# Two-layer cross-attention kernel: project only the first four batches ahead of the first attention, and the other twelve inside it

## The chip, the cores and the metric

One Trainium2 chip, one core. The metric is the device time of one execution of the whole program, in microseconds, lower is better. The engines are TensorE (PE), VectorE (DVE), ScalarE (ACT), GpSimd (POOL) and SyncE (SP); SP computes nothing here and issues most DMAs. A `q` behind a name (SPq, ACTq) means that the engine's queue issues something, a DMA above all.

## The reference

Sixteen batches of 128 tokens with 128 features go through cross-attention with biases (layer 0, 16 heads of 8), a mixture of eight experts, a masked causal cross-attention (layer 1), and a ternary feed-forward part. Only the first layer's attention and what stands ahead of it are touched:

```python
xn = (x - mean) / sqrt(var + eps)          # over the 128 features
q = split_heads(xn @ Wq.T + bq)
k = split_heads(ctx @ Wk.T + bk)
v = split_heads(ctx @ Wv.T + bv)
scores = einsum('bhqd,bhkd->bhqk', q, k) / sqrt(8)
probs = softmax(scores)
x = x + merge_heads(einsum('bhqk,bhkd->bhqd', probs, v)) @ Wo.T + bo
```

The products q·k are wanted in float32 accuracy while TensorE runs bf16. So every projection is split into three bf16 parts: the first is its rounding, the second the rounding of what is left (`rest`), the third what is left then.

## The kernel before

The program is five blocks one after the other, each with a program of its own for each engine; an engine enters a block only when all have left the one before: `context` (line 443), `attention` for layer 0 (line 709), `experts`, `attention` for layer 1, `ternary_ffn`. The order of the work in each is written out by hand.

**`context`** works by groups g of four batches (512 tokens). UNITS lists eight units: the keys and the queries of each group. TensorE projects keys (L655) from the transposed context `ctx_t`, turns the normalised tokens (L636), projects values (L643) and queries (L667). ScalarE copies a turned tile (L684), writes the first part of a unit (L696) and the second part (L689). VectorE measures the tokens (L578), normalises them (L594), forms `rest` (L601), adds the values' bias (L587); for the first queries it also makes parts two and three (L611, L613). GpSimd takes the root (L553) and makes the third part (L558). SyncE stores the parts into `k_dram` (five copies of 128 KB for a unit of keys, since parts one and two are stored twice) and `q_dram` (three), and loads the rows of batches 0 and 1 back (`load_half`, L110 and L113). Three units are stored in this block, the other five at places inside the attention (`LATE`). All weights, those of layer 1 too, are loaded at its start.

**`attention`** runs in steps b from -2 to 17, in the same order on each engine; four slots of `k_rows` and `q_rows` hold the rows of four batches. A step has four quarters q of four heads. In step b TensorE makes, by quarters, the scores of batch b+2 (L868), of which VectorE takes maxima (L958, and a split of them into bf16 parts, L965 to L971), and the shifted scores of batch b (L885), which ScalarE exponentiates (L1040). Behind quarter 0 stand the products with the values of batch b-1 (L899) and the turning of the maxima of batch b+1 (L906). ScalarE copies these (L1052) and SyncE lays them into three rows of `q_rows` by a DMA (`lay_maxima`, L795); the shifted scores of that batch wait for it. The output of batch b-2 is turned, projected (L921, L925) and added to x (L984). Rows of batch b+4 are loaded once the shifted scores of batch b have freed the slot:

```python
def load(b, r):
    for half in range(2):
        sp.wait_ge(shifted, (b - SLOTS) * NQ + (half + 1) * NQ // 2)
        load_half(sp, c, b, r, half)
    lay_maxima(b - 2, (r - 2) % SLOTS)
```

GpSimd puts the values of batch b into `v_aug` (`fill`, L1093), ahead of L899 of that batch. Behind its step 1 it adds the output's bias to all of x (L1115), and VectorE waits for that (`bias_added`) before its step 2.

**Semaphores around the change.** `stored` (here `first_stored`, `parts_stored`, `late_stored`, `last_stored`) stands at 16 per DMA landed; SyncE waits for it before it loads rows of that group. `third_ready` counts third parts, `copied` first parts, `rest_ready` what is left, `second_ready` second parts.

## Time and profile before

| | us |
|---|---|
| time, median of 3 runs | 433.83 (432.37 to 436.69) |
| time of the profiled execution | 434.39 |
| its span, from the first instruction to the last | 432.7 |
| outside the span | 1.69 |

Times of single instructions below are microseconds from the start of the span. The mean granted clock of TensorE over the span is 0.924 of full speed (2.4 GHz); the lower of its two levels is 1.2 GHz. Of the span about 38 us are the context phase and some 96 us the first attention.

### The profile page before, as it was taken

How to read it: one execution, taken by the hardware profiler on the slowest of the kernel's cores; microseconds unless marked ns; L12 is line 12 of the kernel's file. 1: busy time of each engine (PE TensorE's matmuls, PEld its weight loads, DVE VectorE, ACT ScalarE, POOL GpSimd, SP SyncE). 2: the span in 40 equal slices, each digit the busy share in tenths (PEclk: the TensorE clock that was granted, in tenths of full speed). 3: DMA queues.
4: the chain of work that ended last, by engine and by line, in shares of the span. 5: the costliest groups of instructions: out<-in, count | busy, mean ns of one | idle time of the engine just before them, and what ended most of it. 6: DMA issues, size and time to landing. Idle time of an engine off the chain costs nothing. (4 is left out here: it accounts for less than half of the span.)

```text
span 432.7 us, 10420 instructions
## 1 busy us (share of the span) xinstructions
PE 359.2 (83%) x3434; PEld 258.3 (60%) x3434; DVE 288.3 (67%) x905; ACT 224.6 (52%) x420; POOL 90.2 (21%) x163
## 2 busy tenths in 40 slices
PE   2684779887877999999999999799899999756654
PEld 0452667776753677677767777566677676534433
DVE  6765768998946553663442443687789799367993
ACT  2152436665654745434343344055556656648993
POOL 7335131020211102101001001133333343310000
PEclk9886769999996999999999999889999999857996
DMA  7664954433144001630170100113443331000111
GB/s 215 138 157 111 226 165 129 130 117 111 55 124 148 2 2 40 126 80 2 36 208 12 36 0 0 37 31 104 122 127 113 101 100 28 3 1 1 32 30 37
DMA packets 54100, 34.98 MB, mean 81 GB/s; under 512 B 38744, under 2 KB 46256, under 8 KB 54064
## 3 DMA queue, kind: packets, MB, share of 16 engines
q1 hardware_dynamic: 44032, 31.43, 26.8%
q10 hardware_dynamic: 10032, 3.08, 3.0%
q8 instruction: 20, 0.33, 0.3%
q14 instruction: 16, 0.13, 0.1%
HBM read 24.60 MB, written 9.44 MB: 79 GB/s over the span
## 5 line engine op out<-in xcount | busy, mean ns | idle before, releaser
L1040 ACT ACTIVATE probs<-ps_e 128x512 f32<-128x512 f32 x128 | 74.6, 594 | 54.2 <-PE ps_e L885 49.7
L958 DVE TENSOR_REDUCE neg<-ps_s 128x4 f32<-128x512 f32 x128 | 85.1, 684 | 21.6 <-PE ps_s L868 20.1
L1286 DVE SCALAR_TENSOR_TENSOR x_all<-ps_ym,c_g,x_all 128x128 f32 (+1 forms) x128 | 36.0, 344 | 63.2 <-PE ps_ym L1381 63.0
L1381 PEld LDWEIGHTS ps_ym<-w,hid 128*128 128x128 f32 x512 | 60.8, 192 | 9.2 <-issue 6.7
L868 PE MATMUL ps_s<-k_rows,q_rows 96*128 96x128 bf16 x512 | 54.2, 234 | 10.6 <-DVE neg L958 4.9
L1381 PE MATMUL ps_ym<-w,hid 128*128 128x128 f32 x512 | 62.2, 276 | 0.0
L1371 PE MATMUL ps_h<-tok_t,w 128*128 (+1 forms) x128 | 62.1, 608 | 0.0
L1488 ACT ACTIVATE hid<-ps_h,b 128x512 f32<-128x512 f32 x64 | 43.1, 684 | 35.4 <-PE ps_h L1371 34.0
L868 PEld LDWEIGHTS ps_s<-k_rows,q_rows 96*128 96x128 bf16 x512 | 40.1, 104 | 24.1 <-issue 10.0
L885 PE MATMUL ps_e<-q_rows,k_rows 128*128 128x128 bf16 x512 | 51.2, 226 | 3.8 <-DMA q_rows<-neg_t 3.3
L885 PEld LDWEIGHTS ps_e<-q_rows,k_rows 128*128 128x128 bf16 x512 | 37.0, 101 | 9.1 <-DMA q_rows<-neg_t 3.9
L899 PE MATMUL ps_pv<-probs,v_aug 128*32 128x128 f32 x1024 | 36.5, 285 | 0.0
L1371 PEld LDWEIGHTS ps_h<-tok_t,w 128*128 128x128 f32 x128 | 22.6, 195 | 20.1 <-issue 14.9
L1093 POOL TENSOR_TENSOR v_aug<-v_all,zero 128x128 f32<-128x128 f32 x32 | 14.8, 463 | 88.4 <-PE ps_pv L899 87.2
L864 PE MATMUL ps_s<-upper,identb 128*128 128x512 bf16 x64 | 25.8, 403 | 4.6 <-PEq L1138 2.0
L899 PEld LDWEIGHTS ps_pv<-probs,v_aug 128*32 128x32 f32 x1024 | 27.0, 113 | 4.1 <-issue 0.4
L1052 ACT ACTIVATE neg_t<-ps_n 48x128 bf16<-48x128 bf16 x32 | 8.6, 269 | 35.3 <-PE ps_n L906 35.3
L1718 PE MATMUL ps_tf<-ident,gr 128*128 128x128 f32 x64 | 11.3, 303 | 14.2 <-ACT gr L1672 14.2
L925 PE MATMUL ps_y<-attn_w,oo_t 128*128 128x128 f32 x64 | 16.2, 336 | 7.5 <-ACT oo_t L1057 6.8
L984 DVE TENSOR_TENSOR x_all<-ps_y,x_all 128x128 f32<-128x128 f32 (+1 forms) x32 | 9.2, 287 | 16.7 <-PE ps_y L925 16.4
L1102 POOL TENSOR_SCALAR_AFFINE_SELECT probs<-probs 128x512 f32<-128x512 f32 x32 | 20.0, 625 | 0.0
L1045 ACT ACTIVATE o_t<-ps_pv 128x512 f32<-128x512 f32 x32 | 18.6, 580 | 2.1 <-PE ps_pv L899 2.0
(200 smaller groups left out, 555.7 us busy)
## 6 DMA issues: line engine op xcount, KB each, us to landing
k_rows<-k_dram SPq DMA_DIRECT2D x32, 144.0 KB
q_rows<-q_dram SPq DMA_DIRECT2D x32, 144.0 KB
k_rows<-k_dram SPq DMA_DIRECT2D x16, 288.0 KB
q_rows<-q_dram SPq DMA_DIRECT2D x16, 288.0 KB
k_dram<-parts SPq DMA_DIRECT2D x35, 128.0 KB, 2.5
w<-in_w SPq DMA_DIRECT2D x16, 128.0 KB, 2.7
q_dram<-parts SPq DMA_DIRECT2D x15, 128.0 KB, 2.2
q_dram<-parts ACTq DMA_DIRECT2D x9, 128.0 KB, 3.2
```

Source lines behind the costliest of these rows:

```text
L864: pe.matmul(ps_s[:, q % 2, :], identb[:], c["upper"][:].unsqueeze(1).to_broadcast([P, HQ, P]), start=True, stop=False, skip_group_check=True)
L868: last = pe.matmul(ps_s[:, q % 2, j * P:(j + 1) * P], q_rows[0:ROW_MAX, r, h, :], k_rows[0:ROW_MAX, r, h, :], start=(layer == 0), stop=Tru ...
L885: last = pe.matmul(ps_e[:, q % 2, j * P:(j + 1) * P], k_rows[:, r, h, :], q_rows[:, r, h, :], start=not masked, stop=True, skip_group_chec ...
L899: last = pe.matmul(ps_v[VW * j:VW * (j + 1), q * P:(q + 1) * P], v_aug[:, s, q * HQ + j, :], probs[:, s, q, j * P:(j + 1) * P], start=True ...
L958: dve.tensor_reduce(neg[:, s, q * HQ:(q + 1) * HQ], ps_s[:, q % 2, :].rearrange("p (h k) -> p h k", h=HQ), AX_X, ALU.max, negate=True).the ...
L1040: act.activation(probs[:, s, q, :], ps_e[:, q % 2, :], ACT.Exp, scale=SCALE).then_inc(exp_done, 1)
L1045: act.activation(o_t[:, s, :], ps_v[:], ACT.Copy).then_inc(ot_ready, 1)
L1102: pool.affine_select(out=probs[:, s, q, :], in_=probs[:, s, q, :], compare_op=ALU.is_ge, fill=0.0, base=0, pattern=[[0, HQ], [1, P]], chan ...
L1286: dve.scalar_tensor_tensor(out=batch_of(x_all, g * G + j), in0=ps_y[:, e % 2, j * D:(j + 1) * D], scalar=c_g[:, j, e:e + 1], in1=batch_of( ...
L1371: pe.matmul(ps_h[:, m, :], w1[:, e, m * P:(m + 1) * P], tok_t[:, bass.ds(g * GT, GT)], start=True, stop=True).then_inc(h_done, 1)
L1381: last = pe.matmul(ps_y[:, e % 2, j * D:(j + 1) * D], hid[:, (e % 2) * M + m, j * P:(j + 1) * P], w2[:, e, m, :], start=(m == 0), stop=(m ...
L1488: act.activation(hid[:, (e % 2) * M + m, :], ps_h[:, m, :], ACT.Gelu, bias=b1[:, e * M + m:e * M + m + 1]).then_inc(h_ready, 1)
```

## The change

A class `Projections` (`pr`) holds the tensors, semaphores and steps of the projection, so that they live through `context` and the first `attention`. `context` now does the keys and queries of group 0, the values of groups 0 and 1, and the projection of the keys of group 1. The rest is spread over the attention: TensorE does four products ahead of step -2 into banks that the attention doesn't use yet (`ps_e`, `ps_pv`, `ps_y`, `ps_o`), and turns or projections of queries between quarters; ScalarE copies each late unit out of its bank twice (its first part, and in float32 into `rest`), GpSimd subtracts (`leave`) and makes the third part, ScalarE the second. The late units are numbered m = 0 to 5: keys of groups 1, 2, 3, queries of groups 1, 2, 3.

The queries of a group are stored by one DMA of 384 KB in place of three of 128 KB. The rows of batches 1 to 7 are loaded whole, by two DMAs in place of four. The values' bias is added in `fill` and no longer by VectorE. Layer 1's attention weights and the mask go from the start of `context` to the end of SyncE's attention program.

```diff
+LATE_UNITS = (("k", 1), ("k", 2), ("k", 3), ("q", 1), ("q", 2), ("q", 3))
+WHOLE = 2 * SLOTS
...
+    def copy_full(self, act, m, bank):
+        kind, g = LATE_UNITS[m]
+        self.copy_first(act, kind, g, m + 3, bank)
+        wait(act, self.third_ready, m - 3)
+        act.activation(self.rest[:, (m + 2) % 4, :], bank, ACT.Identity, bias=self.bias(kind)).then_inc(self.copied, 1)
...
+    def leave(self, pool, m):
+        kind, g = LATE_UNITS[m]
+        pool.wait_ge(self.copied, 2 + 2 * (m + 1))
+        pool.tensor_tensor(self.remainder(m + 2), self.remainder(m + 2), self.part(kind, g, 0), ALU.subtract)\
+            .then_inc(self.rest_ready, 1)
+    def second(self, act, m):
+        act.wait_ge(self.rest_ready, m + 1)
+        act.activation(self.part(kind, g, 1), self.remainder(m + 2), ACT.Copy).then_inc(self.second_ready, 1)
+    def third(self, pool, m):
+        pool.wait_ge(self.second_ready, m + 1)
+        pool.tensor_tensor(self.part(kind, g, 2), self.remainder(m + 2), self.part(kind, g, 1), ALU.subtract)\
+            .then_inc(self.third_ready, 1)
...
 # context, TensorE
+            pe.matmul(ps_p[:, 0, :], attn_w[:, 0, 1, :], ctx_t[:, 0:GT], start=True, stop=True).then_inc(pr.p_done, 1)
+            pr.turn(pe, 0, ps_x)
+            pr.queries(pe, 0, ps_p[:, 1, :])
+            pr.values(pe, 0, ps_v[:, 0])
+            pr.keys(pe, 1, ps_p[:, 2, :])
+            pr.values(pe, 1, ps_v[:, 1])
 # context, ScalarE
+            pr.copy_first(act, "k", 0, 1, ps_p[:, 0, :])
+            pr.copy_turned(act, 0, ps_x[:])
+            pr.copy_first(act, "q", 0, 2, ps_p[:, 1, :])
+            pr.copy_full(act, 0, ps_p[:, 2, :])
+            pr.copy_values(act, 0, ps_v[:, 0, :])
+            pr.copy_values(act, 1, ps_v[:, 1, :])
 # context, VectorE
+            pr.normalise(dve, 0, STAT_STEPS + 1)
+            pr.leave_first(dve, "k", 0, ps_p[:, 0, :])
+            dve.wait_ge(pr.x_in[1], 16)
+            dve.wait_ge(pr.x_in[2], 16)
+            pr.stats(dve, range(G, B))
+            pr.leave_first(dve, "q", 1, ps_p[:, 1, :])
 # attention, SyncE
+                pr.store_queries(sp, 0)
+                sp.wait_ge(pr.stored[0], 16 * (K_PARTS + 1))
+                for half in range(2):
+                    load_half(sp, c, 0, 0, half)
+                load_whole(sp, c, 1, 1)
+                load_whole(sp, c, 2, 2)
+                lay_maxima(0, 0)
+                load_whole(sp, c, 3, 3)
+                sp.wait_ge(pr.third_ready, 1)
+                pr.store_keys(sp, 1, (0, 3))
+                lay_maxima(1, 1)
+                pr.store_keys(sp, 1, (1, 4, 2))
+                sp.wait_ge(pr.third_ready, 4)
+                pr.store_queries(sp, 1)
+                sp.wait_ge(pr.stored[1], 16 * (K_PARTS + 1))
+                load(4, 0)
+                load(5, 1)
+                pr.store_keys(sp, 2, (0, 3))
+                load(6, 2)
+                pr.store_keys(sp, 2, (1, 4))
+                load(7, 3)
+                pr.store_keys(sp, 2, (2,))
+                sp.wait_ge(pr.third_ready, 5)
+                pr.store_queries(sp, 2)
+                sp.wait_ge(pr.stored[2], 16 * (K_PARTS + 1))
                 for b in range(2 * SLOTS, B):
+                    if b == last * G:
+                        sp.wait_ge(pr.stored[3], 16 * (K_PARTS + 1))
                     load(b, b % SLOTS)
...
+                for m, name in enumerate(("Wq", "Wk", "Wv", "Wo")):
+                    sp.dma_start(attn_w[:, 1, m, :], t["L1_" + name]).then_inc(gate_in, 16)
+                sp.dma_start(c["mask_dram"], c["mask_b"][:]).then_inc(gate_in, 16)
 # attention, TensorE: beside a quarter (step, quarter)
+                (-2, 1): lambda: pr.turn(pe, 2, bank_t),
+                (-1, 1): lambda: (pe.wait_ge(pr.copied, 2 + 2 * 3), pr.queries(pe, 2, bank_q[1])),
+                (-1, 3): lambda: pr.turn(pe, 3, bank_t),
+                (0, 1): lambda: (pe.wait_ge(pr.v_ready, NG), pr.queries(pe, 3, bank_q[2])),
 # attention, VectorE, ahead of its steps
+                pr.variance(dve, G, B, STAT_STEPS + 1)
+                for g in range(1, NG):
+                    pr.normalise(dve, g, 2 * (STAT_STEPS + 1) + (g > 1))
 # attention, ScalarE: behind steps -3, -2, -1 and 0
+            def first_copies():
+                pr.copy_full(act, 1, bank_k[0])
+                pr.copy_values(act, 2, bank_v[0])
+                pr.copy_turned(act, 1, bank_t[:])
+                pr.copy_full(act, 2, bank_k[1])
+                pr.copy_values(act, 3, bank_v[1])
+                pr.copy_full(act, 3, bank_q[0])
+                pr.second(act, 0)
+            def second_copies():
+                pr.copy_turned(act, 2, bank_t[:])
+                pr.second(act, 1)
+                pr.second(act, 2)
+            def third_copies():
+                pr.copy_full(act, 4, bank_q[1])
+                pr.copy_turned(act, 3, bank_t[:])
+            def fourth_copies():
+                pr.second(act, 3)
+                pr.copy_full(act, 5, bank_q[2])
+                pr.second(act, 4)
...
+                if also else {-3: first_copies, -2: second_copies, -1: third_copies, 0: fourth_copies,
+                              1: lambda: pr.second(act, 5), 2: lambda: store_last((0, 3)), 3: lambda: store_last((1, 4)),
+                              4: lambda: (store_last((2,)), pr.store_queries(act, 3))},
 # attention, GpSimd: ahead of its steps, then behind steps -2, 0 and 1
+                for m, later in ((0, 0), (1, 0), (0, 1), (2, 0), (1, 1), (2, 1)):
+                    if later:
+                        pr.third(pool, m)
+                    else:
+                        pr.leave(pool, m)
...
             def add_bias():
+                split_late(5)
+                pool.wait_ge(pr.xn_ready, B)
                 pool.tensor_tensor(x_all[:], x_all[:], c["row_bias"][:, 1, :].unsqueeze(1).to_broadcast([P, B, D]),
                                    ALU.add).then_inc(bias_added, 1)
...
+                else {-2: lambda: split_late(3), 0: lambda: split_late(4), 1: add_bias}, beside)
```

`split_late(m)` is `leave(m)` and then `third(m)`.

ScalarE, from the copy of batch 0's maxima to batch 1's second exponential (`probs0` is written by the exponentials, `neg_t0` by the copy of the maxima, `o_t0` by the copy of the sums). Before:

```order
L1052 ACTIVATE neg_t0<-ps_n0 48x128
L143 DMA k_dram<-parts 128x4x128 x5
L1040 ACTIVATE probs0<-ps_e0 128x512
L1052 ACTIVATE neg_t0<-ps_n0 48x128
L1040 ACTIVATE probs0<-ps_e0 128x512 x4
L1052 ACTIVATE neg_t0<-ps_n0 48x128
L1045 ACTIVATE o_t0<-ps_pv0 128x512
L1040 ACTIVATE probs0<-ps_e0 128x512 x3
```

And now:

```order
L1126 ACTIVATE neg_t0<-ps_n0 48x128
L263 ACTIVATE parts<-ps_e0,attn_bias 128x4x128
L272 ACTIVATE pr_rest<-ps_e0,attn_bias 128x512
L282 ACTIVATE pr_xn_t<-ps_o0 128x512
L1114 ACTIVATE probs0<-ps_e0 128x512
L1126 ACTIVATE neg_t0<-ps_n0 48x128
L1114 ACTIVATE probs0<-ps_e0 128x512 x3
L295 ACTIVATE parts<-pr_rest 128x4x128
L263 ACTIVATE parts<-ps_y0,attn_bias 128x4x128
L272 ACTIVATE pr_rest<-ps_y0,attn_bias 128x512
L295 ACTIVATE parts<-pr_rest 128x4x128
L1114 ACTIVATE probs0<-ps_e0 128x512
```

Four copies now stand between batch 0's last exponential and batch 1's first, and three ahead of batch 0's first.

GpSimd, from the clearing of `v_aug0` to the addition of the bias to x. Before:

```order
L1085 MEMSET v_aug0 128x1024
L1087 MEMSET v_aug0 128x32
L1093 TENSOR_TENSOR v_aug0<-v_all,zero 128x16x8 x3
L1115 TENSOR_TENSOR x_all<-x_all,row_bias 128x2048
L1093 TENSOR_TENSOR v_aug0<-v_all,zero 128x16x8 x4
```

And now:

```order
L1196 MEMSET v_aug0 128x1024
L1198 MEMSET v_aug0 128x32
L288 TENSOR_TENSOR pr_rest<-pr_rest,parts 128x512
L301 TENSOR_TENSOR parts<-pr_rest,parts 128x4x128
L1207 TENSOR_TENSOR v_aug0<-v_all,row_bias 128x16x8 x2
L288 TENSOR_TENSOR pr_rest<-pr_rest,parts 128x512
L301 TENSOR_TENSOR parts<-pr_rest,parts 128x4x128
L1207 TENSOR_TENSOR v_aug0<-v_all,row_bias 128x16x8
L288 TENSOR_TENSOR pr_rest<-pr_rest,parts 128x512
L301 TENSOR_TENSOR parts<-pr_rest,parts 128x4x128
L1236 TENSOR_TENSOR x_all<-x_all,row_bias 128x2048
L1207 TENSOR_TENSOR v_aug0<-v_all,row_bias 128x16x8 x4
```

The splits of the queries of groups 1, 2 and 3 (L288 and L301, m = 3, 4, 5) now stand ahead of the first `fill`, ahead of the third, and ahead of the addition to x.

SyncE's queue, in the changed kernel, from the rows of batch 7 to the maxima of batch 6 (`q_rows<-neg_t0` lays maxima). The whole rows of batch 7 are the first two rows, the halves of batch 8 stand behind the stores:

```order
L155 DMA k_rows<-k_dram 72x1x2048
L158 DMA q_rows<-q_dram 72x1x2048
L816 DMA q_rows<-neg_t0 3x16x128
L210 DMA k_dram<-parts 128x4x128
L214 DMA q_dram<-parts 128x12x128
L110 DMA k_rows<-k_dram 72x1x1024
L113 DMA q_rows<-q_dram 72x1x1024
L110 DMA k_rows<-k_dram 72x1x1024
L113 DMA q_rows<-q_dram 72x1x1024
L816 DMA q_rows<-neg_t0 3x16x128
```

Before, nothing stands between the maxima of batch 5 and the rows of batch 8. The two stores of group 2, and SyncE's wait for them, now stand there.

## Rows read from the trace of the kernel before

**Rows 1.** Windows of context and attention: length, busy us of five engines, clock, DMA, GB/s.
```profile
0.00:38.00 38.00, 19.40 (x66) 11.61 (x67) 23.78 (x62) 13.21 (x21) 18.22 (x31) 0.88 0.59 151
38.00:134.00 96.00, 76.16 (x1155) 61.76 (x1156) 75.51 (x236) 49.73 (x112) 18.20 (x25) 0.89 0.49 138
```

**Rows 2.** Timeline of the context phase: start, length, engine, line, what, count, idle before.
```profile
13.17 1.91 PE L667 MATMUL ps_p<-xn_t,attn_w 128*128 128x512 f32 x2
13.32 2.42 DVE L578 BATCH_NORM_STATS2 st_all<-x_all 128x6 f32<-128x128 f32 x12 [2.88 <-DMA x_all<-in_x]
...
19.18 1.49 SPq L143 DMA_DIRECT2D q_dram<-parts  x3
...
20.88 1.09 DVE L594 TENSOR_SCALAR xn<-x_all,mean,rstd 128x128 f32<-128x128 f32 x4
...
22.37 0.96 SPq L110 DMA_DIRECT2D k_rows<-k_dram  x1
...
26.31 2.88 DVE L594 TENSOR_SCALAR xn<-x_all,mean,rstd 128x128 f32<-128x128 f32 x4
...
27.91 1.12 PE L667 MATMUL ps_p<-xn_t,attn_w 128*128 128x512 f32 x2 [0.46 <-ACT xn_t L684]
...
35.32 2.26 POOL L558 TENSOR_TENSOR parts<-rest,parts 128x512 bf16<-128x512 f32 x2 [1.75 <-ACT parts L689]
...
37.93 1.01 PE L868 MATMUL ps_s<-k_rows,q_rows 96*128 96x128 bf16 x8 [3.93 <-PEq L448]
```

**Rows 3.** Groups on ScalarE, 0 to 80 us: a second part; count, busy us, mean ns.
```profile
L689 ACT ACTIVATE parts<-rest 128x512 bf16<-128x512 f32 x7 | 4.4, 625 | 1.2 <-DVE rest L601 1.1
```

**Rows 4.** Timeline of the first attention, from the first exponential to step 2.
```profile
46.84 0.60 ACT L1040 ACTIVATE probs<-ps_e 128x512 f32<-128x512 f32 x1 [3.98 <-PE ps_e L885]
...
49.51 0.60 ACT L1040 ACTIVATE probs<-ps_e 128x512 f32<-128x512 f32 x1 [0.26 <-PE ps_e L885]
...
51.76 0.80 SPq L110 DMA_DIRECT2D k_rows<-k_dram  x1
...
52.00 0.45 POOL L1093 TENSOR_TENSOR v_aug<-v_all,zero 128x128 f32<-128x128 f32 x1 [11.76 <-PE ps_pv L899]
...
52.41 4.51 POOL L1115 TENSOR_TENSOR x_all<-x_all,row_bias 128x2048 f32<-128x2048 f32 x1
...
54.53 2.42 DVE L965 CAST neg_parts<-neg 128x16 bf16<-128x16 f32 x1
...
55.67 0.40 PE L868 MATMUL ps_s<-k_rows,q_rows 96*128 96x128 bf16 x4 [1.68 <-DMA q_rows<-q_dram]
...
57.46 0.61 PE L885 MATMUL ps_e<-q_rows,k_rows 128*128 128x128 bf16 x4 [1.40 <-DMA q_rows<-neg_t]
...
57.99 0.68 DVE L958 TENSOR_REDUCE neg<-ps_s 128x4 f32<-128x512 f32 x1
...
61.01 0.63 PE L868 MATMUL ps_s<-k_rows,q_rows 96*128 96x128 bf16 x4
```

**Rows 5.** Windows, 58 to 63 us: length, busy us of five engines, clock, DMA, GB/s.
```profile
58.00:63.00 5.00, 5.00 (x56) 4.41 (x56) 2.34 (x5) 2.71 (x6) 0.46 (x1) 0.50 0.56 153
```

**Rows 6.** Timeline, steps 4 to 6: first shifted scores of steps 4 and 6; maxima laid.
```profile
68.48 0.39 PE L885 MATMUL ps_e<-q_rows,k_rows 128*128 128x128 bf16 x4
...
70.59 0.76 SPq L795 DMA_DIRECT2D q_rows<-neg_t  x1
...
75.07 0.76 SPq L795 DMA_DIRECT2D q_rows<-neg_t  x1
...
77.72 0.39 PE L885 MATMUL ps_e<-q_rows,k_rows 128*128 128x128 bf16 x4
```

**Rows 7.** The page, part 6: a store's DMA, its size, us from issue to landing.
```profile
q_dram<-parts SPq DMA_DIRECT2D x15, 128.0 KB, 2.2
```

**Rows 8.** Timeline, end of the attention: SyncE's last DMA, TensorE's first of the experts.
```profile
130.62 0.43 SPq L137 DMA_DIRECT2D w<-in_w  x1
...
133.54 1.08 PE L1348 MATMUL ps_q<-ident,tok_tk 128*128 128x128 f32 x4 [1.24 <-PEq L716]
```

431 lines of the change are left out of this document (212 added, 219 removed).

## The prediction

> **What bounds the kernel now.** I read the windows by stage first, then the timeline of the first 80 us engine by engine, then groups for durations, and the waits where the timeline showed gaps. The windows say how much the change can touch: 38 us of context and 96 us of attention [rows 1]. In the context no engine is full: VectorE, the busiest, works 23.8 of 38 us, TensorE 19.4. It is a chain. VectorE waits for the twelve later batches of x and measures them (13.32, 2.42 us) before it splits the first queries, stored from 19.18; the first rows are fetched from 22.37; GpSimd's last third parts end at 37.58, and only then can the attention begin, at 37.93 [rows 2]. Rows of batches 0 and 1 had long been fetched by then. The first exponential starts at 46.84. Steps 1 to 3 have waits of their own: TensorE waits for rows of batch 4 until 55.67, for batch 2's maxima until 57.46, VectorE for x until 57.99 [rows 4]. TensorE comes back at the low clock: 58 to 63 us shows a granted clock of 0.50 with TensorE busy for all 5 us [rows 5]. From 68.48 the attention has its pace: two steps take 77.72 - 68.48 = 9.24 us [rows 6], or 4.62 each, in which VectorE and TensorE are both nearly full. Time saved at the start counts only if it is still there at 68.48, and time lost after that is lost.
>
> **The change, step by step.** I carry five marks through it.
>
> 1. *Attention begins.* The first queries no longer wait behind the values, and VectorE's splitting ends near 17. Last to leave the context is now ScalarE, which copies group 1's keys twice and two banks of values. TensorE's products (two of 512 columns are 1.91 us at the low clock, 1.12 at the high one [rows 2]) give 19.8, between 18.5 and 20.5, against 37.9. But the first queries' store moves behind this point.
>
> 2. *First exponential.* Before, three query stores from 19.18 had landed when the rows were fetched at 22.37, 3.2 us [rows 2]. One DMA of the same 384 KB: 3.2 to 4, I take 3.6, so fetching starts at 23.4. A half fetched from 51.76 was there at 55.67, 3.9 us [rows 4]: scores at 27.3. TensorE's four products, a turn and a projection ahead of them end between 27 and 29.2, by the clock. Before, scores to exponential took 46.84 - 37.93 = 8.9 us [rows 2, 4]. It gets 0.8 longer: group 2's turning stands between quarters, and ScalarE reaches the copy of the maxima behind `second(2)`, which waits for GpSimd's three subtractions. 27.3 + 8.9 + 0.8 = 37.0 (36.2 to 39), 9.8 ahead of before.
>
> 3. *VectorE goes on into step 2.* Here the 9.8 us go. Before, the exponential at 46.84 was followed by VectorE's step 2 at 57.99, 11.15 us later [rows 4]. Now: four exponentials, 3.3 us before (46.84 to 50.11 [rows 4]), plus one projection at the low clock, 1.9: 5.2. Then ScalarE does `second(3)`, 0.63 [rows 3]; GpSimd `third(3)`, 1.13 (two in 2.26 [rows 2]), two fills of 0.45 [rows 4], `leave(4)`, 1.13; ScalarE `second(4)`, 0.63: 4.4 us, with batch 1's exponentials queued behind it on ScalarE, and TensorE's values of batch 0 behind the first fill. ScalarE's `copy_full(5)` lies beside GpSimd and is free. Batch 1's exponentials, about 4.3. Then `second(5)` 0.63, `third(5)` 1.13 and the addition to x, 4.51 [rows 4], for which VectorE waits: 6.3. Sum 5.2 + 4.4 + 4.3 + 6.3 = 20.2: 37.0 + 20.2 = 57.2, against 57.99. At the high clock it is 18.5, with slower splits 21.5. Rows of batch 4 don't decide: `third(3)` at about 44, store and wait 3.6, fetch 3.9 give 51.5, and batch 2's maxima, laid behind them in the same queue, come near 52.
>
> 4. *Step 4.* Before, after 57.99 VectorE had to wait for a late TensorE: the third quarter's scores began at 61.01 [rows 4]. Now TensorE has done that work while VectorE waited, and starts it one maximum later, 57.2 + 0.7 = 57.9: 3.1 earlier. But TensorE has then stood for over 3 us and is at the low clock for 5 us from 57.9 rather than the 2 that were left at 61.01; 3 us more at half speed cost 1.2 (0 to 1.5). Step 4 starts 1.9 us earlier.
>
> 5. *Step 6.* SyncE lays batch 5's maxima at 70.59 of the old times, and batch 6's at 75.07, with four fetches between [rows 6]. Now behind the first stand two stores, 0.5 us each by the 1.49 for three, and a wait until they land: from the query store 3.2 [rows 2], between 2.2 by [rows 7] and 4. 70.59 + 0.76 + 0.5 + 3.2 = 75.05; four fetches of 0.8: 78.2. Batch 6's maxima are laid 3.2 late, and in the old times TensorE needed them by 77.72, with at most 0.2 to spare: a stall of 3.0 (1.5 to 4). What it does to the clock: the old waits around 55.67 and 57.46 were of this shape, and the two steps behind them took 68.48 - 57.46 = 11.0 us against 9.24, 1.8 more. I take 1.3, as the clock may stay.
>
> Smaller: six DMAs on ScalarE between steps 2 and 5 delay exponentials and the next copy of maxima, partly in ScalarE's idle time (it is busy half of the attention [rows 1]): 0.5 (0 to 1.5). Five more DMAs of about 0.48 on SyncE at the end: it stopped at 131.05, the experts began at 133.54 [rows 8], so 2.4 us just fit: 0.2 (0 to 1). The bias in `fill` replaces an addition of zero: nothing. Later blocks do the same work.
>
> Sum: -1.9 + 3.0 + 1.3 + 0.5 + 0.2 = **+3.1**, and 434.39 + 3.1 = **437.5**. The profiled execution lies 0.6 above the median of the three, within their spread, so I leave it so.
>
> A price from a page, aside: the Trainium skill, page "DMA: Bandwidth & Descriptors", section on the anatomy of one DMA, gives a fixed 2.0 us and the bytes at 436 GB/s; an estimate by it for 384 KB is 2.9 us. The row for 128 KB has 2.2 us, near what the rule gives. By it the stall of mark 5 would be 0.3 less.
>
> **Rivals.** *The gain is kept.* TensorE stays at the high clock through the first steps: mark 2 is 36.2, mark 3 takes 18 rather than 20.2, so VectorE goes on at 54.2 and step 4 starts 5 to 6 us earlier; the stores land in 2.2 us, so step 6 stalls 2 us and the clock stays. -5.5 + 2 + 0.3 = -3.2, or 431; with stores hidden whole 429. For it: TensorE has four products at once at 19.8. Against: before, 37.9 to 49 went at the low clock with much the same work, and stalls there are many.
>
> *VectorE and GpSimd in each other's way, slower.* Four normalisations took 1.09 us at 20.88 and 2.88 at 26.31, beside GpSimd's third parts, and a cast of 16 columns took 2.42 us, until GpSimd's addition was over [rows 2, 4]. Now twelve normalisations and the casts of batches 0 to 3 lie beside twelve subtractions of GpSimd. Eight normalisations at 0.72 rather than 0.28 end near 29.5 rather than 26; it decides where they end later than the scores at 27.3, and costs 2 there; casts that wait for a subtraction cost up to 1.1 for each batch, 2 in all. 437.5 + 4 = 441.5. Against it: GpSimd often waits for ScalarE. The Trainium skill, page "SBUF — State Buffer", says the two share a port pair under an exclusive lock, so that the later one is blocked for the other's whole instruction; the cast's 2.42 us agrees, and by the rule each wait is a whole subtraction, as priced.
>
> **How the numbers follow.** A measurement of this kernel can tell about 1%, 4.3 us. The forecast has 0.45, the first rival 0.25, the second 0.30. Faster by over 1% (below 429.5) is 0.17, from the first alone. Within 1%: 0.33 of the forecast, 0.08 and 0.04 of the rivals, 0.45. Slower by over 1% (above 438.2): 0.12 of the forecast and 0.26 of the second, 0.38. The range is 430 to 443: the first rival's 431 below; above, 441.5 and the upper bound of the stall.
>
> **What would show it.** In the changed profile: attention from about 20, first exponential near 37; ScalarE waiting some 2.5 us for GpSimd's `rest` between batches 0 and 1; VectorE's step 2 just behind GpSimd's addition to x, near 57; TensorE waiting for laid maxima once, in step 6, some 9 us behind step 4. I am wrong if the first exponential is before 35, if the addition to x ends before 54, or if step 6 has no wait: then it is faster. If the normalisations end past 29, the second rival holds.

## The result and the profile after

| | us |
|---|---|
| kernel before, median of 4 runs | 434.38 (432.37 to 436.69) |
| changed kernel, median of 4 runs | 440.79 (437.12 to 441.85) |
| ratio, with its 95% interval | 1.0115 [1.0071, 1.0158] |
| measured again (6 and 29 runs) | 438.81 against 434.62, 1.0103 [1.0065, 1.014] |
| its profiled execution, span | 437.12, 435.4 (before 434.39, 432.7) |

About 1% slower. The ratio and its interval come from the single executions and aren't the quotient of the two medians. Executions that fell in a slower state (two of halves below, three of stores, one each of second3 and v4, and a few of before) are left out of the ratios and kept in the medians.

Here and below, "19.14 for 37.93" means 19.14 in this kernel where the other one has 37.93. The profiled execution was the fastest of the first four and lies 2.7 us above the profiled one of before; the medians differ by 6.4 and 4.2. The changed kernel scatters more: measured again, its six runs go from 435.43 (mean granted clock 0.928) to 441.46 (0.906).

The timeline of the changed kernel, the start of the attention (columns as in [rows 2]), shows how early the attention starts now:

```profile
19.14 1.10 PE L240 MATMUL ps_e<-ctx_t,attn_w 128*128 128x512 f32 x2 [1.69 <-PEq L607]
...
37.62 0.60 ACT L1114 ACTIVATE probs<-ps_e 128x512 f32<-128x512 f32 x1
...
43.70 1.93 PE L944 MATMUL ps_pv<-probs,v_aug 128*32 128x128 f32 x32 [2.08 <-POOL v_aug L1207]
```

The attention begins at 19.14 for 37.93 [rows 2], the first exponential at 37.62 for 46.84 [rows 4]. A step's first values can be followed from one kernel to the next; they begin at these times, with the experts' first matmul in the last column:

| kernel | step 1 | 2 | 3 | 4 | 5 | 6 | 7 | 16 | experts |
|---|---|---|---|---|---|---|---|---|---|
| before | 50.80 | 58.00 | 64.19 | 68.80 | 73.42 | 78.05 | 82.74 | 126.80 | 133.54 |
| changed | 43.70 | 52.90 | 58.64 | 64.38 | 70.31 | 77.85 | 83.55 | 127.15 | 135.16 |
| changed - before | -7.1 | -5.1 | -5.6 | -4.4 | -3.1 | -0.2 | +0.8 | +0.4 | +1.6 |

Of the 18.8 us at the attention's start 9.2 are left at the first exponential and 5.6 at step 3: most of it goes where the projections now stand. Steps 3 to 6 give back the rest: from step 4 to step 7 it takes 19.2 us, before 13.9. The waits of TensorE for batches' rows, and SyncE's queue beside the last of them, in the timeline of the changed kernel:

```profile
51.93 0.61 PE L909 MATMUL ps_s<-k_rows,q_rows 96*128 96x128 bf16 x4 [3.75 <-DMA q_rows<-q_dram]
...
63.82 0.40 PE L909 MATMUL ps_s<-k_rows,q_rows 96*128 96x128 bf16 x4 [1.00 <-DMA q_rows<-q_dram]
...
69.75 0.40 PE L909 MATMUL ps_s<-k_rows,q_rows 96*128 96x128 bf16 x4 [1.28 <-DMA q_rows<-q_dram]
...
76.40 0.39 PE L909 MATMUL ps_s<-k_rows,q_rows 96*128 96x128 bf16 x4 [2.00 <-DMA q_rows<-q_dram]
77.41 0.52 PE L930 MATMUL ps_e<-q_rows,k_rows 128*128 128x128 bf16 x4 [0.61 <-DMA q_rows<-neg_t]
```

```profile
67.25 1.00 SPq L214 DMA_DIRECT2D q_dram<-parts  x1
71.43 0.79 SPq L110 DMA_DIRECT2D k_rows<-k_dram  x1
...
74.78 0.77 SPq L816 DMA_DIRECT2D q_rows<-neg_t  x1
```

The first fence reads: rows of batches 4, 6, 7 and 8 are late, and batch 6's laid maxima by another 0.61 us. The second: from the issue of group 2's query store to the next fetch SyncE passes 4.2 us, and batch 6's maxima are laid four fetches later, at 74.78. The windows of the changed kernel, and those of before below them (length, busy us of PE, PEld, DVE, ACT, POOL, clock, DMA share, GB/s):

```profile
58.00:70.00 12.00, 8.97 (x154) 7.38 (x152) 9.76 (x30) 6.85 (x15) 0.91 (x2) 1.00 0.83 207
70.00:82.00 12.00, 8.66 (x130) 6.89 (x128) 6.80 (x19) 5.44 (x13) 0.91 (x2) 0.86 0.59 157
```

```profile
58.00:70.00 12.00, 11.62 (x179) 9.93 (x179) 8.00 (x24) 6.87 (x15) 0.92 (x3) 0.79 0.48 137
70.00:82.00 12.00, 10.83 (x173) 9.05 (x173) 10.92 (x34) 8.21 (x19) 1.36 (x3) 1.00 0.44 131
```

In 58 to 70 the DMA engines are busy 0.83 of the time where they were 0.48: SyncE and ScalarE now issue ten stores of groups 2 and 3 there, beside the fetches, where the kernel before had issued its last store by 57.4. TensorE, with a better clock (1.00 for 0.79), works 8.97 us for 11.62. It waits.

And at the end, in the timeline of the changed kernel, SyncE's last DMA is 3.6 us later than in [rows 8], and TensorE stands 2.77 for 1.24 before the experts:

```profile
134.22 0.43 SPq L137 DMA_DIRECT2D w<-in_w  x1
...
135.16 1.09 PE L1470 MATMUL ps_q<-ident,tok_tk 128*128 128x128 f32 x4 [2.77 <-PEq L735]
```

### The profile page after: what moved, and what is told of

Its sections match the earlier page's. It is cut to its first block and busy times, and to the rows that moved or that the text cites. A ratio compares the mean times of both kernels' runs of the same rounds, so it can differ in the third digit from the quotient of the medians.

```text
span 435.4 us, 10400 instructions
## 1 busy us (share of the span) xinstructions
PE 358.9 (82%) x3432; PEld 258.9 (59%) x3434; DVE 283.8 (65%) x897; ACT 229.3 (53%) x429; POOL 96.1 (22%) x168
## 5 line engine op out<-in xcount | busy, mean ns | idle before, releaser
L909 PE MATMUL ps_s<-k_rows,q_rows 96*128 96x128 bf16 x512 | 53.9, 233 | 14.2 <-DMA q_rows<-q_dram 11.4
L930 PE MATMUL ps_e<-q_rows,k_rows 128*128 128x128 bf16 x512 | 50.7, 224 | 1.2 <-DMA q_rows<-neg_t 0.6
L944 PE MATMUL ps_pv<-probs,v_aug 128*32 128x128 f32 x1024 | 38.0, 293 | 2.1 <-POOL v_aug L1207 2.1
L944 PEld LDWEIGHTS ps_pv<-probs,v_aug 128*32 128x32 f32 x1024 | 28.0, 116 | 6.5 <-POOL v_aug L1207 2.2
L1840 PE MATMUL ps_tf<-ident,gr 128*128 128x128 f32 x64 | 12.2, 322 | 12.7 <-ACT gr L1794 12.7
L960 PE MATMUL ps_o<-ident,o_t 128*128 128x128 f32 x128 | 19.6, 277 | 0.0
```

Of the source, the lines that this page charges most:

```text
L909: last = pe.matmul(ps_s[:, q % 2, j * P:(j + 1) * P], q_rows[0:ROW_MAX, r, h, :], k_rows[0:ROW_MAX, r, h, :], start=(layer == 0), stop=Tru ...
L930: last = pe.matmul(ps_e[:, q % 2, j * P:(j + 1) * P], k_rows[:, r, h, :], q_rows[:, r, h, :], start=not masked, stop=True, skip_group_chec ...
L944: last = pe.matmul(ps_v[VW * j:VW * (j + 1), q * P:(q + 1) * P], v_aug[:, s, q * HQ + j, :], probs[:, s, q, j * P:(j + 1) * P], start=True ...
L1840: last = pe.transpose(ps_t[:, s, k * P:(k + 1) * P], gr[:, s, k * P:(k + 1) * P], ident[:])
```

## The experiments

All were timed beside the kernel before on their chip. Medians in us; ratios to the kernel before. Four chips were used (after_again to stores; all3 to v2_act; fill, v3 and v4; v5), so kernels of different groups are compared by their ratios.

The expectations weigh three theories. S: SyncE's order of stores and fetches gives the gain back. C: TensorE's clock gives it back, whatever the order. V: VectorE and GpSimd hold each other up.

| kernel | median | ratio [95%] |
|---|---|---|
| after_again, the changed kernel | 438.81 | 1.0103 [1.0065, 1.014] |
| tail | 436.08 | 1.0032 [1.0012, 1.0052] |
| halves | 437.91 | 1.005 [1.0017, 1.0084] |
| stores | 435.30 | 1.0003 [0.997, 1.0036] |
| all3 | 435.91 | 1.0019 [0.9992, 1.0047] |
| second3 | 436.33 | 1.0033 [1.0003, 1.0064] |
| v2 | 429.37 | 0.989 [0.9848, 0.9932] |
| v2_act | 432.70 | 0.9955 [0.9924, 0.9986] |
| fill | 440.44 | 1.0111 [1.0075, 1.0146] |
| v3 | 433.38 | 0.9976 [0.994, 1.0012] |
| v4 | 433.55 | 0.9966 [0.9938, 0.9994] |
| v5 | 430.87 | 0.9893 [0.9853, 0.9933] |

**after_again** is the changed kernel, unedited.

> The changed kernel itself once more, on the chip of the next three, so that each has its own measure. Two theories stand against each other in this series. Theory S (SyncE's order): the first phase does bring its gain (step 4 began 4.4 us earlier than before), and it is given back later through what SyncE's queue now holds: whole loads for batches 4 to 7, group 2's stores with the wait for their landing in step 6, and five weight and mask DMAs behind the last step. Theory C (clock): the gain is given back because TensorE's granted clock falls in more places, so that the order of SyncE's queue hardly matters. For this run both expect the same: a ratio of 1.007 to 1.016 to the kernel before. In the profile S expects the marks of the first profile to come back within 0.5 us (step 4 at 64.1, step 6 at 77.4, experts' first matmul at 135.2), and C expects them to move with the low stretches of the clock, by 1 us or more.

Step 4's values began at 65.08 for 64.38, step 6's at 78.17 for 77.85, the experts at 135.16 again. The first phase repeats within a microsecond, though step 4 is 0.7 us off, more than theory S allowed. But step 16 began at 128.72 for 127.15, and TensorE then stood only 1.26 us before the experts: the 1.6 us vanished in the wait for SyncE's tail.

**tail**: the five DMAs spread over the loads.

```diff
-                for m, name in enumerate(("Wq", "Wk", "Wv", "Wo")):
-                    sp.dma_start(attn_w[:, 1, m, :], t["L1_" + name]).then_inc(gate_in, 16)
-                sp.dma_start(c["mask_dram"], c["mask_b"][:]).then_inc(gate_in, 16)
 # in the loop over b from 2 * SLOTS, behind load(b, b % SLOTS)
+                    if 10 <= b < 14:
+                        name = ("Wq", "Wk", "Wv", "Wo")[b - 10]
+                        sp.dma_start(attn_w[:, 1, b - 10, :], t["L1_" + name]).then_inc(gate_in, 16)
+                    if b == 14:
+                        sp.dma_start(c["mask_dram"], c["mask_b"][:]).then_inc(gate_in, 16)
```

> The five DMAs (four weights of the second attention and the mask) that the change put behind SyncE's last maxima are spread over the loads of batches 10 to 14, where SyncE has idle time; nothing else changes. Theory S: the experts' first matmul follows the end of attention as closely as before the change, 1.5 us earlier than in the repeated run of the changed kernel (133.6 for 135.2), and the time falls by 1.5 us (438.9 where the changed kernel has 440.4). Theory C, and the 0.2 us that the prediction gave this tail: no change beyond 0.3 us.

Timeline of tail, its end:

```profile
131.64 0.43 SPq L137 DMA_DIRECT2D w<-in_w  x1
...
132.98 1.09 PE L1472 MATMUL ps_q<-ident,tok_tk 128*128 128x128 f32 x4 [1.24 <-PEq L735]
```

The wait is 1.24 again, as before the change. The time fell by 2.7 us (438.81 - 436.08), more than the 1.5 of this wait; in the profile the experts begin 2.2 us earlier. The intervals allow 1.5. The tail was no 0.2 us.

**halves**: batches 4 to 7 fetched in halves.

```diff
-WHOLE = 2 * SLOTS
+WHOLE = SLOTS
...
-                if layer == 0 and q == 2 and not isinstance(b, int):
+                if layer == 0 and q == 2 and (not isinstance(b, int) or b >= WHOLE):
```

> Batches 4 to 7 are fetched in halves again, as batches 8 and on are; batches 1 to 3 stay whole. Theory S: the first scores of batch 6 and of batch 7 no longer wait for rows (1.00 us at 63.8 and 1.28 us at 69.7 in the changed kernel's profile), steps 3 and 4 last 4.7 to 5.0 us for 5.7 and 5.9. But SyncE's wait for group 2's stores stands where it did, behind the wait for step 3's scores, so that of the 2.2 us some 1 to 2 arrive at step 6, and the time falls by 1 to 2 us if that wait moves forward with the steps, by nothing if the wait sits at its old place. Theory C: steps 3 and 4 keep their length within 0.3 us, and the time does not move.

About 2 us by the ratios, 0.9 by the medians, with overlapping intervals: no gain is shown. The profiled execution took 441.54, so only the kind of its waits is read. At step 4 a wait for rows became one for laid maxima:

```profile
63.83 0.40 PE L930 MATMUL ps_e<-q_rows,k_rows 128*128 128x128 bf16 x4 [0.98 <-DMA q_rows<-neg_t]
```

SyncE issues them at 60.24, as early as in the changed kernel (60.29), behind four fetches instead of two; why they are not there before 63.83 isn't shown. From one step's values to the next, steps 3 and 4 last 5.9 and 5.5 us, not the 4.7 to 5.0 expected.

**stores**: group 2's six stores together.

```diff
-                load(5, 1)
-                pr.store_keys(sp, 2, (0, 3))
-                load(6, 2)
-                pr.store_keys(sp, 2, (1, 4))
-                load(7, 3)
-                pr.store_keys(sp, 2, (2,))
-                sp.wait_ge(pr.third_ready, 5)
-                pr.store_queries(sp, 2)
 # behind the two row DMAs of load(5, 1), ahead of its lay_maxima(3, 3):
+ # keys (0, 3, 1, 4, 2) of group 2, wait for third_ready 5 and store_queries(sp, 2)
                 load(6, 2)
                 load(7, 3)
```

> All six of group 2's stores are issued together, right behind the fetch of batch 5 at about 50.5 us where SyncE waits 4.9 us for batch 3's maxima, instead of being spread over the loads of batches 5 to 7. They have then long landed when batch 8 is fetched. Theory S: no wait for the stores' landing ahead of batch 8 (4.2 us at 67.3 in the changed kernel), batch 6's maxima are laid at about 70.5 instead of 74.8, the 2.0 us wait for rows at 76.4 and the 0.6 us for the maxima go, the clock stays high in step 6, and step 7 begins 2.5 to 4 us earlier (80 for 83.2); the time falls by 3 us. Theory C: the wait goes, but the time falls by 0.5 us or less, since the clock falls elsewhere.

The largest single gain, 3.5 us, near theory S, but by another way through the steps. Timeline of stores, SyncE and TensorE:

```profile
64.13 0.79 SPq L155 DMA_DIRECT2D k_rows<-k_dram  x1
...
67.44 0.79 SPq L110 DMA_DIRECT2D k_rows<-k_dram  x1
```

```profile
71.65 0.61 PE L906 MATMUL ps_s<-k_rows,q_rows 96*128 96x128 bf16 x4 [2.56 <-DMA q_rows<-q_dram]
```

Batch 8's fetch begins at 67.44 for 71.43: the wait for the landing is gone. Batch 7's rows, fetched from 64.13, now land only after 7.5 us, beside group 3's stores and batch 8's fetch, and a wait of 2.56 stands ahead of step 5. Batch 6's maxima are issued at 75.10 for 74.78, not at the 70.5 expected. Step 6's values begin 0.2 us later than in the changed kernel, step 7's 0.8 us earlier, not the 2.5 to 4 expected, and the experts 0.6 us earlier, at 134.56 after a wait of 2.92. So the run shows what the new order gives, and the profile accounts, at step 7, for 0.8 us of the 3.5.

**all3**: tail, halves and stores together, no other line.

> The three edits of the first series in one kernel: the five DMAs off the end of SyncE's queue, batches 4 to 7 in halves, group 2's stores together behind the fetch of batch 5. Alone they gave 0.7, 0.5 and 1.0 per cent against the changed kernel. Theory S: they act on three different places and so add up in part; with the stores' wait gone, the gain of the halves is no longer taken back at step 6. Ratio to the kernel before 0.988 to 0.994 (429.5 to 432). Theory C: whatever of these stalls goes, the clock takes about the same share elsewhere; the sum is no better than the best single edit, ratio 1.000 or more.

Missed: 1.0019, no better than stores alone, as theory C would have it. The timeline of all3 gives a cause that lies in SyncE's queue:

```profile
53.90 3.52 SPq L210 DMA_DIRECT2D k_dram<-parts  x5
57.46 0.53 SPq L214 DMA_DIRECT2D q_dram<-parts  x1
58.04 1.38 SPq L816 DMA_DIRECT2D q_rows<-neg_t  x1
...
62.72 0.61 PE L929 MATMUL ps_e<-q_rows,k_rows 128*128 128x128 bf16 x4 [3.75 <-DMA q_rows<-neg_t]
```

Four more fetches of 0.8 us (the halves of batches 4 and 5) push the stores from 50.7 to 53.9, into the time when batch 3's maxima are due. These are laid at 58.04 for 56.02 in stores, and TensorE waits 3.75 us: it has them 4.7 us after their issue. Step 3's values begin at 63.25, 3.3 us later than in stores. Two edits, of which stores alone pays and halves may, collide in one queue. This is read from the profile; no run tests it by itself.

**second3**: one instruction of ScalarE.

```diff
             def third_copies():
+                pr.second(act, 3)
...
             def fourth_copies():
-                pr.second(act, 3)
```

> One instruction of ScalarE is moved: the second part of group 1's queries is taken at about 34.3 us, where ScalarE is idle, instead of behind the exponentials of batch 0 at 41.4. GpSimd, which stood waiting for it 7.8 us with the fill of batch 0's values behind it, should go on at 35; the first values begin 2 us earlier (41.7 for 43.7), group 1's queries are stored 1.4 us earlier (41.9 for 43.3, as SyncE's three key stores now decide), and batch 4's rows come 1.4 us earlier (50.5 for 51.9). Theory S: 1 to 1.5 us of this reach step 3, and then the waits for whole loads and for group 2's stores stand where they stood relative to the steps, so all moves forward: 1 us faster than the changed kernel (ratio 1.007 to 1.009). Theory C: no change within 0.5 us. Rival V (VectorE and GpSimd in each other's way): GpSimd's part now falls beside VectorE's splits of batch 1, which take longer by 1 us, and batch 1's maxima come later: nothing gained or slower.

2.5 us below the changed kernel's median, and 0.7% by the ratios: more than theory S's 1 us. The profile shows less, the experts at 134.30 for 135.16. Step 1's values begin at 43.00, not the 41.7 expected; step 2's 8.21 us after them, for 9.20. Rival V leaves a small trace: the first cast of batch 1's split takes 0.78 us for 0.17, beside GpSimd's `leave`, but TensorE waits for that split no longer than before (0.69 for 0.73).

**v2** puts group 1's and 2's stores ahead and takes group 3's to SyncE; it holds tail, halves and second3.

```diff
 # SyncE's new order; the lines of the old order are left out
                 load_whole(sp, c, 2, 2)
+                sp.wait_ge(pr.third_ready, 1)
+                pr.store_keys(sp, 1, (0, 3, 1, 4, 2))
                 lay_maxima(0, 0)
                 load_whole(sp, c, 3, 3)
                 sp.wait_ge(pr.third_ready, 4)
                 pr.store_queries(sp, 1)
+                pr.store_keys(sp, 2, (0, 3, 1))
+                lay_maxima(1, 1)
+                pr.store_keys(sp, 2, (4, 2))
                 sp.wait_ge(pr.stored[1], 16 * (K_PARTS + 1))
                 load(4, 0)
                 sp.wait_ge(pr.third_ready, 5)
                 pr.store_queries(sp, 2)
+                load(5, 1)
+                pr.store_keys(sp, 3, (0, 3, 1, 4, 2))
+                sp.wait_ge(pr.third_ready, 6)
+                pr.store_queries(sp, 3)
+                load(6, 2)
+                load(7, 3)
```

> Everything found so far in one kernel: the five DMAs spread, batches 4 to 7 in halves, ScalarE's move of the last kernel, group 1's key copies stored in SyncE's idle time before batch 0's maxima, group 1's queries at 36 us, group 2's keys around batch 1's maxima, group 2's queries ahead of the fetch of batch 5, and group 3's six stores behind it, on SyncE instead of ScalarE. Theory S: batch 4's rows no longer wait for the store (its landing ends at about 39.5) but for batch 0's slot, free at 41.4, so they come at about 46 for 51.9; step 2 begins at 48 to 49 for 52.3 and step 6 at 68 to 70 for 77.4, less what fetches and stores lose to each other. Ratio 0.978 to 0.988 (425 to 429). Theory C: 0.995 or above.

429.37: 5.1 us faster than the kernel before, 9.4 than the changed one. Step 1's values begin at 42.27, step 2's at 47.83, step 6's at 71.92 (changed kernel: 43.70, 52.90, 77.85). Step 6 comes 2 us later than theory S had it, and the ratio lies just outside its range. The largest wait left, from the timeline of v2 (GpSimd, then TensorE):

```profile
47.87 4.53 POOL L1239 TENSOR_TENSOR x_all<-x_all,row_bias 128x2048 f32<-128x2048 f32 x1
```

```profile
53.27 0.59 PE L913 MATMUL ps_s<-k_rows,q_rows 96*128 96x128 bf16 x4 [3.62 <-DVE neg L1036]
```

VectorE stands until GpSimd's addition to x is done, TensorE behind it.

**v2_act** leaves group 3's stores on ScalarE.

```diff
 # v2 with these lines out, and ScalarE's store_last at steps 2, 3 and 4 as in the changed kernel
-                pr.store_keys(sp, 3, (0, 3, 1, 4, 2))
-                sp.wait_ge(pr.third_ready, 6)
-                pr.store_queries(sp, 3)
```

> The same as the kernel before it in this series, but group 3's six stores stay on ScalarE, as in the changed kernel. It measures what these six DMAs cost on ScalarE, which the prediction put at 0.5 us, against what they cost on SyncE. Theory S: ScalarE's issue time (0.37 to 0.95 us a pair) shows as waits of TensorE for the turned output (0.47 us at 67.1 and 73.0 in the changed kernel) and for nothing else; SyncE in turn is free of 3 to 4 us of issue at 52 to 56 us, where batch 3's maxima are due, so the two kernels lie within 0.5 per cent of each other. The rival, that ScalarE's DMAs are the larger part of the loss: this kernel is slower than the other by 1 per cent.

0.65% slower than v2, with overlapping intervals: between the two expectations. In the profiles the gap is 2.2 us at step 16 (122.58 for 120.35), and 1.8 of it stands already at step 1 (44.06 for 42.27), ahead of any instruction in which the two differ. There the windows differ in the clock, and TensorE has got less far; first v2, then v2_act:

```profile
38.00:42.00 4.00, 2.93 (x32) 2.05 (x33) 3.21 (x8) 2.57 (x6) 0.00 (x0) 1.00 1.03 239
```

```profile
38.00:42.00 4.00, 3.50 (x20) 2.29 (x21) 1.74 (x6) 1.31 (x3) 0.00 (x0) 0.52 0.98 236
```

But the clock isn't all that differs. Step 1's values wait for batch 1's maxima, and SyncE lays them at 39.66 in v2 and at 41.50 in v2_act, behind three key stores whose issue took 3.25 and 4.25 us:

```profile
36.37 3.25 SPq L210 DMA_DIRECT2D k_dram<-parts  x3
39.66 0.78 SPq L816 DMA_DIRECT2D q_rows<-neg_t  x1
```

```profile
37.20 4.25 SPq L210 DMA_DIRECT2D k_dram<-parts  x3
41.50 0.78 SPq L816 DMA_DIRECT2D q_rows<-neg_t  x1
```

TensorE waits for them in both (0.66 and 0.59 us), and in both SyncE had issued without a gap since 28.6, waiting for no engine. So the 1.8 us lie in SyncE's issues (0.3 at 28.6, 0.6 in the five key stores that start there, 1.0 in these three), and a high clock would not have brought v2_act's step 1 forward; why the same issues take longer is open. For ScalarE's six DMAs the profiles leave 0.4 us; the medians don't settle it.

**fill**: 32 transposes ahead of the wait for batch 4's rows.

```diff
+                if layer == 0 and q == 0 and isinstance(b, int) and b == 4:
+                    for _ in range(32):
+                        pe.transpose(ps_n[:, 2 * P:3 * P], identb[:], identb[:])
```

> The changed kernel with 32 extra transposes of a constant (into an unused part of the bank of the turned maxima) that TensorE works off before it waits for batch 4's rows, where it stood idle 3.75 us and after which its granted clock was low until 57.2. Nothing else waits for them. They take 3 us or less of the idle time, so the first scores of batch 4 still begin when the rows land, at about 52. Theory C: the clock stays high through step 2, whose matmuls then last 0.39 us for 0.63, and step 3 begins 0.7 to 1.5 us earlier than in the changed kernel (57 for 58.3), and all that follows with it: ratio 1.006 to 1.009 instead of 1.0103. Theory S: step 2 becomes shorter too, but the later stalls (whole loads, the wait for group 2's stores) are set by SyncE, and take 0.5 us or more of it back: ratio 1.008 to 1.0103. Nothing gained at all would mean that the low clock of step 2 is not the price of that wait.

Nothing gained. TensorE in the timeline of fill:

```profile
48.53 1.95 PE L893 MATMUL ps_n<-identb 128*128 128x128 bf16 x32
53.26 0.40 PE L912 MATMUL ps_s<-k_rows,q_rows 96*128 96x128 bf16 x4 [2.79 <-DMA q_rows<-q_dram]
...
54.91 0.63 PE L912 MATMUL ps_s<-k_rows,q_rows 96*128 96x128 bf16 x4
```

They fill 1.95 us and leave 2.79 idle. The scores after the wait are still quick (0.40), but those from 54.91 on are slow (0.63): the fall comes later, it isn't prevented. Step 2 lasts 5.56 us (values to values) for 5.74, and batch 6's rows are waited for 2.83 us where it was 1.00. Batch 4's rows themselves came 1.3 us later than in the changed kernel (53.26 for 51.93), for a reason that isn't known. So this fits theory S, but as the clock was hardly held and the rows came late, it doesn't measure what a held clock would give.

**v3**: v2 with the bias before step 0.

```diff
             def add_bias():
-                split_late(5)
...
-                else {-2: lambda: split_late(3), 0: lambda: split_late(4), 1: add_bias}, beside)
+                else {-2: lambda: split_late(3), -1: add_bias, 0: lambda: split_late(4), 1: lambda: split_late(5)}, beside)
```

> The best kernel so far (ratio 0.989) with one more edit: GpSimd adds the bias to x before step 0 of the attention, where it stood idle for 5.6 us, instead of after step 1, and splits the last group's queries then. In the best kernel's profile VectorE waits 5.07 us for x at the start of step 2, TensorE behind it 3.62 us at 53.3, and the clock is low from 53.3 to 58.7. Theory S (a wait taken away uncovers the next one, but each of them is worth its length): the wait goes, step 3 begins at about 53 for 57.3, less what SyncE's 3.4 us of group 3's stores now holds up; ratio 0.979 to 0.984. Rival V: GpSimd's 4.5 us now fall beside VectorE's maxima and splits of batches 1 and 2, which take longer, and what was won at step 2 is lost at steps 0 and 1: ratio 0.987 or more. Theory C: 0.988 or more.

Rival V, plainly: 4 us slower than v2 (0.9% by the ratios). GpSimd, VectorE and TensorE in the timeline of v3:

```profile
36.73 4.50 POOL L1237 TENSOR_TENSOR x_all<-x_all,row_bias 128x2048 f32<-128x2048 f32 x1
```

```profile
37.64 3.62 DVE L1043 CAST neg_parts<-neg 128x16 bf16<-128x16 f32 x1
41.30 0.17 DVE L1045 TENSOR_TENSOR neg_rest<-neg,neg_parts 128x16 f32<-128x16 f32 x1
```

```profile
42.99 0.29 PE L955 MATMUL ps_n<-identb,neg_parts 128*128 128x128 bf16 x1 [4.71 <-DVE neg_parts L1049]
```

A cast of 16 columns ends at 41.26, right behind GpSimd's addition (41.23), and TensorE waits 4.71 us for this split, where v2 has 1.34. Step 1's values begin at 48.38 for 42.27.

**v4**: v3 with GpSimd out of the way of batch 0's split.

```diff
 # GpSimd: v_aug is cleared ahead of third(0); then
+                pr.third(pool, 0)
+                pr.leave(pool, 2)
+                pool.wait_ge(neg_ready, 1)
+                pr.third(pool, 1)
+                pr.third(pool, 2)
 # SyncE
+                pr.store_keys(sp, 1, (0, 3))
                 lay_maxima(0, 0)
                 load_whole(sp, c, 3, 3)
+                pr.store_keys(sp, 1, (1, 4, 2))
```

> The kernel before it in this series, with GpSimd's work moved out of the way of VectorE's split of batch 0's maxima: the two clearings of v_aug come before it, where GpSimd is idle, and the third parts of groups 2 and 3's keys wait until that split is done. Of group 1's key copies three are stored behind the fetch of batch 3 instead of before batch 0's maxima. In all profiles of the changed kernel the three operations of this split that stand beside GpSimd take 0.6 to 1.1 us instead of 0.17. Rival V: they take 0.17 to 0.2 again, the split is ready 2 us earlier, batch 0's maxima are laid at 31.5 for 33.3 and the first exponential comes 1 to 1.4 us earlier (35.6 for 36.9): ratio 0.003 lower than the kernel before it. Theory S: the split is shortened, but rows of batch 1 (landing at 30.8) set the queries of group 2 and with them the first exponential, so 1 us is the most that can arrive. If the three operations keep their length, GpSimd is not what makes them long.

The split, first in the changed kernel, then in v4:

```profile
30.25 0.62 DVE L1039 CAST neg_parts<-neg 128x16 bf16<-128x16 f32 x1
30.91 1.08 DVE L1041 TENSOR_TENSOR neg_rest<-neg,neg_parts 128x16 f32<-128x16 f32 x1
32.02 0.85 DVE L1043 CAST neg_parts<-neg_rest 128x16 bf16<-128x16 f32 x1
```

```profile
29.82 0.17 DVE L1044 CAST neg_parts<-neg 128x16 bf16<-128x16 f32 x1
30.03 0.17 DVE L1046 TENSOR_TENSOR neg_rest<-neg,neg_parts 128x16 f32<-128x16 f32 x1
30.24 0.17 DVE L1048 CAST neg_parts<-neg_rest 128x16 bf16<-128x16 f32 x1
```

GpSimd is what made them long: 0.17 each with it waiting. In the changed kernel TensorE had waited 1.27 us for this split (at 33.14); in v4 that wait is gone. But batch 1's rows, which theory S named, came at 33.06 (32.14 in v3, 31.26 in the changed kernel; why so late is open), so what the shorter split is worth wasn't measured. 433.55 is v3's time within its interval.

**v5**: v2 with the bias between the splits.

```diff
             def add_bias():
-                split_late(5)
+                pr.leave(pool, 5)
+                pool.wait_ge(neg_ready, SLOTS)
...
                 pool.wait_ge(bias_added, 1)
+                pr.third(pool, 5)
 # VectorE: the wait for bias_added ahead of step 2 becomes one ahead of residual(0), in its last quarter
```

> The kernel with ratio 0.989 once more, with the bias put where VectorE's splits are not: GpSimd starts it as soon as batch 3's maxima are split (46.8 us) and before the third part of group 3's queries (1.1 us earlier than in that kernel), and VectorE waits for it only ahead of the first residual, in the last quarter of step 2, instead of ahead of the whole step. The last run but one showed what it costs beside a split: a cast of 128x16 that takes 0.17 us alone took 3.62 beside it. Theory V and S together: no split is longer than 0.2 us between 36 and 50, VectorE waits 1 to 2.5 us for 5.07 and TensorE 1 to 2 for 3.62, and step 3 begins 1.5 to 2.5 us earlier (55 to 56 for 57.3); ratio 0.983 to 0.988. If the wait only moves (VectorE held at the residual as long as it was held at the step's start), the ratio stays at 0.989 within its interval. Slower than 0.992 would mean that group 3's queries, now ready later, hold SyncE up in front of batch 6's fetch.

At step 2 the waits went as expected: VectorE waits 1.03 us for x (5.07 in v2), and step 2 lasts 5.37 us for 9.47. The next two steps took it all back: step 3 lasts 8.01 us for 5.39, step 4 6.37 for 4.76. Besides, step 1 had begun 1.4 us later than v2's (43.63 for 42.27), ahead of the edit, so step 4's values begin at 62.41 for 62.69 and step 5's at 68.78 for 67.45. One split was longer than the 0.2 us expected: a cast at 37.60 took 0.77, beside GpSimd's `leave`. Timeline of v5, TensorE:

```profile
60.27 0.40 PE L913 MATMUL ps_s<-k_rows,q_rows 96*128 96x128 bf16 x4 [1.77 <-DMA q_rows<-q_dram]
61.88 0.61 PE L934 MATMUL ps_e<-q_rows,k_rows 128*128 128x128 bf16 x4 [1.21 <-DMA q_rows<-neg_t]
```

Batch 6's rows are fetched behind group 3's six stores (52.02 to 55.36 on SyncE), and TensorE, ahead of them now, waits; behind the wait its matmuls are slow until 67.7 (0.63 us for four scores). A ratio of 0.9893 for 0.989.

## Why the prediction was right, and where it was not

The forecast was 437.5 (430 to 443), +3.1 on the profiled execution. That execution came out at +2.7, the medians at 440.79 and 438.81: inside the range, above the forecast. Within 1% had a chance of 0.45, slower by more 0.38; the measured 1.15 and 1.03% lie a little beyond that border, with intervals on both sides of it.

**Mark 1** held: 19.14 for 19.8.

**Mark 2** held by luck: 37.62 for 37.0. Batch 0's rows were there at 26.60, 0.7 us before the 27.3 given. But from scores to exponential it took 11.0 us, not 9.7. The 0.8 us of that sum had the wrong reason: ScalarE was free when the maxima came (it had waited 3.18 us). TensorE had waited 1.94 us for batch 1's rows and then 1.27 for VectorE's split:

```profile
31.26 0.61 PE L909 MATMUL ps_s<-k_rows,q_rows 96*128 96x128 bf16 x4 [1.94 <-DMA q_rows<-q_dram]
33.14 0.29 PE L951 MATMUL ps_n<-identb,neg_parts 128*128 128x128 bf16 x1 [1.27 <-DVE neg_parts L1045]
```

**Mark 3** was 2.1 us pessimistic: VectorE went on into step 2 at 55.06, not 57.2, and batch 4's third-quarter scores began at 55.91, not 57.9. The mechanism was right, VectorE stood for GpSimd's addition to x:

```profile
55.06 1.29 DVE L1032 TENSOR_REDUCE neg<-ps_s 128x4 f32<-128x512 f32 x2 [5.05 <-POOL x_all L1236]
```

Of its four terms the two with GpSimd's splits came out within 0.1 us (4.5 for 4.4, 6.3 for 6.3). The two with exponentials were too large: 3.8 for 5.2 and 2.9 for 4.3. The first was made for a low clock, and TensorE had the high one from 38 to 42 (a window's clock of 1.00), so the projection took 1.08 us, not 1.9.

**Mark 4** failed in its size: 4.4 us ahead at step 4, not 1.9. Of the 2.5 us, 2.0 came in with mark 3. The rest fits the clock, high again at 57.65 (0.39 us for four scores, 0.63 until then), as TensorE's wait, 3.75 us for batch 4's rows, lay at 48.2 to 51.9, earlier than I had put it. "Rows of batch 4 don't decide" was right for VectorE, which stood for x 3.1 us longer. But they, and not VectorE, are what TensorE stood for, and behind that wait its clock was low until 57.6.

**Mark 5** named the right wait on SyncE, and its sum came out nearly right in the wrong parts. From step 5 to 6 the kernel lost 2.9 us to before, for 3.0, and from 6 to 7 1.0, for 1.3. But SyncE's wait, from the issue of the query store to the next fetch, was 4.2 us where 3.2 was given, and the prediction's other estimate, 2.9 us, was further off. TensorE's stall was 2.00 us for batch 8's rows, which the mark doesn't name, and 0.61 for the laid maxima, which it does; it came 13 us behind step 4, not 9. From step 4 to 5 it lost 1.3 us, where the sum had only 0.5, for ScalarE's DMAs. The term left out is the cost of whole fetches and shared DMA engines: TensorE waited 1.28 us for batch 7's rows, and 1.00 for batch 6's ahead of step 4 already (DMA share 0.83 for 0.48). From step 4 to step 7 the changed kernel lost 5.2 us to before, where the sum had 3.0 + 1.3 + 0.5 = 4.8. The run stores shows that SyncE's order is worth 3.5 us of the median. That this is the wait's price isn't shown, since the edit moved six stores and its profile has another wait in the same stretch.

**The tail** was mis-sized most in proportion: 0.2 was given. SyncE ended 3.6 us later, of which the five DMAs are 2.7, and 1.5 us of it was waited for in the profile; tail got 2.7 us of the median back. "2.4 us just fit" was wrong in both numbers. In the run tail SyncE ended at 132.07, 0.9 us ahead of the experts, and TensorE's wait was the 1.24 us of [rows 8]; in the changed kernel it ended at 134.65, 0.5 us ahead of them, and the wait was 2.77. By that an estimate of SyncE's slack before the change is 133.54 - 131.05 - 0.5 = 2.0 us, and 3.6 - 2.0 is the 1.6 us by which the experts came later.

So the +3.1 came out as +2.7 by errors that cancel: -2.5 at step 4, +0.4 from there to step 7 (5.2 for 4.8), -0.4 from step 7 to 16, +1.1 in the tail, and +1.1 in the blocks behind the attention, where I had given nothing. The two profiles of the changed kernel differ by 1.7 us in these blocks (300.2 and 298.5 us from the experts' first matmul to the end of the span, 299.2 before), so the last +1.1 is within their scatter. That the total came within 0.4 us is luck.

**The first rival**, the gain kept, was half right: step 4 came 4.4 us early, but it gave SyncE's stores 2.2 us to land, and 0.3 to all the rest, whole fetches and tail included. v2 shows that it can be kept when the queue is laid out for it. **The second rival** had the mechanism and the wrong place. Its own sign failed: the eight normalisations ended at 26.7, not past 29:

```profile
22.92 3.82 DVE L235 TENSOR_SCALAR pr_xn<-x_all,mean,rstd 128x128 f32<-128x128 f32 x8 [0.60 <-POOL rstd L229]
```

In the changed kernel batch 0's split took 2.8 us for 0.8, and TensorE waited 1.27 us for it; what that cost isn't measured, since in v4 batch 1's rows came late. v3 showed what a split beside the addition to x costs: TensorE waited 4.71 us for it, where v2 has 1.34. The Trainium skill, page "SBUF — State Buffer", section "SBUF: two separate sides", says that the loser of the shared port pair blocks for the other's whole instruction; the trace agrees (cast end 41.26, addition end 41.23).

**Theory C**, that the clock gives back whatever is gained, fell with tail, stores and v2. A part stays: in the changed kernel the slower executions have the lower mean clock (435.43 us with 0.928, 441.46 with 0.906), and up to step 1 the profiles of v2 and v2_act, with the same instructions, have a clock of 1.00 and 0.52 in 38 to 42; but there SyncE's queue, not the clock, made the 1.8 us. What decides the clock was not found. Nor is it settled why the median of the changed kernel lies further above before (4.2 to 6.4 us) than its profile (2.7), or why the medians of tail, stores and second3 fell by 2.5 to 3.5 us where their profiles have the experts' first matmul only 2.2, 0.6 and 0.9 us earlier.

## What to carry to other kernels

When work is moved behind a point where others wait for it, list per queue what each DMA now stands in front of: here 18.8 us won at the attention's start were 5.6 at step 3, and these were spent in steps that wait for one queue, which lays maxima, fetches rows and stores, in program order. The same work in another order was 9.4 us faster, about 2%. Edits that pay alone must be tried together, for they may fill the same gap (all3), and a wait removed uncovers the next one (v5). Large work for GpSimd goes where VectorE has no casts or additions out of SBUF on the critical path, not merely into GpSimd's own idle time (v3). And a sum that comes out right must be checked mark by mark: this one had errors of up to 2.5 us that cancelled.

## What the runs showed of the hardware

A cast of 128x16 on VectorE took 0.17 us alone and 3.62 beside a GpSimd addition of 128x2048; beside GpSimd's clearing of v_aug one took 0.85. Reductions out of the scores' bank were not touched: in v5 they took 0.68 and 1.29 for two beside the same addition, as elsewhere:

```profile
48.62 0.68 DVE L1036 TENSOR_REDUCE neg<-ps_s 128x4 f32<-128x512 f32 x1
50.54 1.29 DVE L1036 TENSOR_REDUCE neg<-ps_s 128x4 f32<-128x512 f32 x2 [1.23 <-PE ps_s L913]
```

```profile
48.30 4.53 POOL L1241 TENSOR_TENSOR x_all<-x_all,row_bias 128x2048 f32<-128x2048 f32 x1 [1.63 <-DVE neg_parts L1049]
```

A whole fetch landed 5.5 us after its first issue (46.43 to 51.9), and 7.5 us beside stores and another fetch; a store of 384 KB was waited for 3.2 us at 19.11, with no other in flight, and 4.2 at 67.25, behind group 2's last key copy (3.7 in after_again). The issue of a key store took SyncE 0.44 us at 66.76 in the changed kernel, 0.57 (five in 2.85) in v2 and 0.85 (five in 4.24) in stores, right behind the fetch of batch 5; what makes the difference wasn't tested.
